# Expert lists written to DRAM by indirect DMAs in place of one-hots and their products, in a two-expert-per-token kernel on Trainium2

## The reference

```
x = x + layernorm(attention(layernorm(x)))
xf = layernorm(x)                         # 4096 x 256
shared = (silu(xf @ sg.T) * (xf @ su.T)) @ sd.T
probs = softmax(xf @ gate_w.T)            # 8 experts
topw, topi = top_k(probs, 2); topw /= topw.sum()
routed = sum over e of  ffn_e(xf) * weight of e for the token (0 if e is not chosen)
x = x + layernorm(shared + routed)        # hidden size of each expert 704
```

## Time and profile before

| | |
|---|---|
| median of 3 runs | 873.82 us (873.72 to 875.32) |
| profiled execution | 874.38 us, of which the span of instructions 872.6 us |
| PE / DVE / ACT / POOL busy | 785.9 / 586.8 / 486.2 / 290.8 us |
| mean granted TensorE clock | 0.978 |
| batches 1 to 6 | about 42.9 us each |
| last batch, from 332.10 to 364.70 | 32.6 us |
| TAIL to the first routed tile | 364.70 to 420.10 us |
| 39 routed tiles and the end | 420.1 to 872.6 us |

### The profile page before, as it was taken

One profiled execution on the slowest core, in us unless ns is written; L12 is line 12 of the kernel. 1 busy time (PEld: TensorE's weight loads), 2 busy tenths in 40 slices (PEclk: granted clock), 3 DMA queues, 4 the chain that ended last, 5 costly groups with the idle time before them and its releaser, 6 DMA issues.

```text
span 872.6 us, 21123 instructions
## 1 busy us (share of the span) xinstructions
PE 785.9 (90%) x6605; PEld 634.1 (73%) x6606; DVE 586.8 (67%) x1585; ACT 486.2 (56%) x1062; POOL 290.8 (33%) x316
## 2 busy tenths in 40 slices
PE   2689999999999998666799999999999999999991
PEld 1346677777777766554588888888888888888880
DVE  7368797979797977898577644455555555555552
ACT  1255757574848486632266655565656565656562
POOL 3010000000010100034255555555555555555542
PEclk9989999999999999999899999999999999999995
DMA  4105262636363634330334454646464646464633
GB/s 187 48 25 188 74 205 75 199 84 195 74 200 91 183 85 140 100 82 19 80 57 68 74 98 76 123 75 146 73 145 73 145 73 145 73 143 74 145 42 94
DMA packets 115747, 93.25 MB, mean 107 GB/s; under 512 B 76816, under 2 KB 107280, under 8 KB 114512
## 3 DMA queue, kind: packets, MB, share of 16 engines
q1 hardware_dynamic: 100704, 71.60, 28.3%
q0 software_dynamic: 14976, 20.78, 16.0%
HBM read 48.70 MB, written 27.39 MB: 87 GB/s over the span
## 4 chain that ended last, share of the span: by engine, by line
PE 72%; DVE 17%; ACT 5%; issue 3%; DMA 2%; POOL 1%; ACTq 0%; SPq 0%; DVEq 0%; POOLq 0%
PE ps L910 40%; PE ps L925 18%; PE ps L981 5%; PE ps L1016 3%; DVE wgu L1270 3%; PE ps L975 2%; DVE hf L1210 2%; ACT wgu L772 2%; DVE wdn L1270 1%; PE ps L986 1%; DVE hT L1220 1%; DVE st L1382 1%; DVE wdn L1515 1%; PE ps L1020 1%; ACT silu L724 1%
## 5 line engine op out<-in xcount | busy, mean ns | idle before, releaser
L910 PE MATMUL ps<-xhl,wgu 128*128 128x256 f16 x3102 | 384.9, 274 | 12.7 <-DMA xhl<-attw 6.7
L910 PEld LDWEIGHTS ps<-xhl,wgu 128*128 (+1 forms) x3102 | 302.7, 98 | 54.5 <-issue 8.6
L1210 DVE SCALAR_TENSOR_TENSOR hf<-ps,sc,silu 128x256 f32<-128x256 f32 x330 | 159.6, 484 | 194.5 <-ACT silu L724 165.3
L925 PE MATMUL ps<-wdn,hT 128*128 (+1 forms) x1870 | 254.9, 273 | 13.6 <-DVE hT L1220 11.2
L724 ACT ACTIVATE silu<-ps,sc 128x256 f32<-128x256 f32 x275 | 130.0, 473 | 233.4 <-PE ps L910 233.2
L925 PEld LDWEIGHTS ps<-wdn,hT 128*128 128x128 f16 x1870 | 179.8, 98 | 40.6 <-DVE hT L1220 13.4
L673 POOL DMA_INDIRECT acc_d<-ysb,gst x78 | 128.9, 1652 | 44.5 <-POOL gst L669 30.9
L606 POOL TENSOR_TENSOR rstd<-ve,mhalf 128x4 f32<-128x4 f32 (+1 forms) x32 | 30.6, 959 | 315.5 <-DVE ve L1195 293.1
L738 ACT CAST hT<-hf 128x256 f16<-128x256 f32 x275 | 109.4, 398 | 14.4 <-DVE hf L1210 11.8
L1220 DVE TENSOR_TENSOR hT<-hf,hT 128x256 f16<-128x256 f32 x275 | 114.7, 417 | 1.7
L662 POOL DMA_INDIRECT attw<-xn_d,gst x78 | 80.5, 1032 | 44.4 <-POOL gst L658 32.6
(11 more groups left out here) (241 smaller groups left out, 753.2 us busy)
## 6 DMA issues: line engine op xcount, KB each, us to landing
wgu<-in_gu SPq DMA_DIRECT2D x8, 1408.0 KB, 6.1
att<-in_x SPq DMA_DIRECT2D x16, 512.0 KB, 5.4
wdn<-in_dn SPq DMA_DIRECT2D x8, 768.0 KB, 8.5
x_d<-att SPq DMA_DIRECT2D x8, 512.0 KB, 2.9
xn_d<-wgu SPq DMA_DIRECT2D x8, 512.0 KB, 3.4
acc_d<-ysb SPq DMA_DIRECT2D x16, 256.0 KB, 2.3
att<-x_d SPq DMA_DIRECT2D x8, 512.0 KB, 4.7
att<-acc_d SPq DMA_DIRECT2D x7, 512.0 KB
```

The costliest lines, as they stand in the source:

```text
L910: ins = te.matmul(o, slot_gu(slot, hw, k, j), x(hx, k), start=(n == 0), stop=(n == len(TERMS) - 1))
L925: ins = te.matmul(y_bank(u, tt), h(hh), slot_dn(slot, c, hw), start=(c == 0 and n == 0 and tt == 0), stop=(c == FC - 1 and n == 1 and tt = ...
L1210: v.scalar_tensor_tensor(out=hf[lo:P, c % 2 * TW:(c % 2 + 1) * TW], in0=up, scalar=scale_of(slot, 1, lo, P), in1=silu[lo:P, c % 2 * TW:(c ...
```

## The change

Token numbers are written to lists in DRAM. `list_d` has for each expert a list with room for all 4096 tokens, and blocks of padding behind. At the start it is filled with numbers of padding rows (4 DMAs from SP), and `xn2_d` gets 256 padding rows.

- Routing goes in three parts (PART): token tiles 0 to 15 in batch 4, 16 to 27 at the beginning of batch 7, 28 to 31 in TAIL. `ranks` on PE gives a token's rank among its expert's tokens: one fp32 product with `upper`, one with `ones` for each earlier batch's counts and one for each tile of the part but the last (1 + 0 + 15, 1 + 4 + 11 and 1 + 7 + 3 products). `route_places` on DVE adds the list's start and takes each choice's place.
- `put_on_lists` on POOL: for each of the 32 token tiles two indirect DMAs that write 128 token numbers of 4 bytes (64 in all). They stand in batches 5 and 6, in batch 7 and in TAIL.
- The first tile of each expert has fixed places in its list: SP reads these eight tiles' numbers with two DMAs when all 64 writes have landed. The numbers of the 31 later tiles are gathered by POOL, four indirect DMAs behind each scatter of tiles 2 to 9 (three behind the last of them).
- The order of the tiles is worked out on DVE during routed tiles 0 to 2 (`ordering`). `idx` serves gather and scatter.
- One-hots, inversion, `route_slots` to `route_indices` are gone. START, ORDER, LAST_ORDER and TAIL are written anew; the steps of the batches stay the same apart from the new ones.

The core of the diff:

```diff
+LAST_ORDER = [("ctx",), ("route_probs", 1), ("G", 0), ("G", 1), ("route_top1", 1), ("G", 2), ("H", 0), ("route_top2", 1), ("route_ranks", 1),
+         ("ctx_out",), ("G", 3), ("route_places", 1), ("H", 1), ("list", 1, 16), ("H", 2), ("D", 0), ("list", 1, 17), ("H", 3), ("H", 4),
+         ("list", 1, 18), ("G", 4), ("D", 1), ("channel_stats",), ("group_mean",), ("G", 5), ("list", 1, 19), ("group_var",), ("H", 5),
+         ("ctx_norm",), ("list", 1, 20), ("H", 6), ("D", 2), ("list", 1, 21), ("list", 1, 22), ("G", 6), ("H", 7), ("H", 8), ("G", 7),
...
-PROGRAM += [(b, step) for b in range(1, B - 1) for step in ORDER if b < NPRE or not step[0].startswith("prep")]
+PROGRAM += [(b, step) for b in range(1, B - 1) for step in ORDER
+            if (b < NPRE or not step[0].startswith("prep")) and (b == PART_IN or not step[0].startswith("route"))
+            and (step[0] != "list" or b == PART_IN + 1 + step[2] // (2 * NT))]
...
+            sp.wait_ge(fill_made, 1)
+            blocks = list_d.rearrange("(n c) o -> n (c o)", c=TW)
+            sp.dma_start(blocks[0:P, :], fill[:, 0:TW]).then_inc(list_filled, 16)
+            sp.dma_start(blocks[P:EMPTY + NTILE, :], fill[0:EMPTY + NTILE - P, 0:TW]).then_inc(list_filled, 16)
+            for t in range(TT):
+                sp.dma_start(xn2_d[TOK + t * P:TOK + (t + 1) * P, :], fill.bitcast(F32)).then_inc(list_filled, 16)
...
+                store_weights(n)
+
+
+            first_tiles = list_d[0:E * TOK, :].rearrange("(e n p h) o -> p e n (h o)", e=E, p=P, h=TT)[:, :, 0, :]
+            idx3 = idx[:, 0:E * TT].rearrange("p (i h) -> p i h", h=TT)
+            sp.wait_ge(listed, 16 * 2 * NTB)
+            sp.dma_start(idx3[:, 0:2, :], first_tiles[:, 0:2, :]).then_inc(idx_first, 16)
+            sp.dma_start(idx3[:, 2:E, :], first_tiles[:, 2:E, :]).then_inc(idx_rest, 16)
...
+            def put_on_lists(n, j):
+
+                pool.wait_ge(places_made, n + 1)
+                if j == 0:
+                    pool.wait_ge(list_filled, 4 * 16)
+                passed(pool)
+                for m in range(2):
+                    at = m * NTB + j
+                    g.indirect_dma_start(list_d, bass.IndirectOffsetOnAxis(ap=posi[:, at:at + 1], axis=0), tok_i[:, j:j + 1], None).then_inc(listed, 16)
 
...
+            def idx_of(i):
+
+                g.indirect_dma_start(idx[:, i * TT:(i + 1) * TT], None, list_d.rearrange("(n h) o -> n (h o)", h=TT),
+                                     bass.IndirectOffsetOnAxis(ap=table[:, i - E:i - E + 1], axis=0)).then_inc(idx_late, 16)
+
             for i in range(E + GROUP):
+                if i + 3 >= E:
+                    pool.wait_ge(idx_late, 16 * (i + 4 - E))
                 gather_x(i + 3, (i + 1) % 2, False)
                 scatter(i)
+                if i == 2:
+                    pool.wait_ge(table_made, 1)
+                    passed(pool)
+                for n in range(E + 4 * (i - 2), min(E + 4 * (i - 1), NTILE)):
+                    if i >= 2:
+                        idx_of(n)
+            pool.wait_ge(idx_late, 16 * (NTILE - E))
             with pool.Fori(0, B - 2) as b:
                 for j in range(GROUP):
...
+            def ranks(n):
+
+                a, b = PART[n]
+                pe.wait_ge(m_made, n + 1)
+                m = part_arrays(n)[4].rearrange("p (t e) -> p t e", e=E)
+                at = max_ps[:, 2 * P:2 * P + (b - a) * E].rearrange("p (t e) -> p t e", e=E)
+                te.matmul(at, upper[:, :], m, start=True, stop=False)
+                for c in range(a // NT):
+                    te.matmul(at, ones[:, :], picks[:, c * E:(c + 1) * E].rearrange("p (o e) -> p o e", o=1).to_broadcast([P, b - a, E]), start=False, stop=False)
+                for j in range(b - a - 1):
+                    ins = te.matmul(at[:, j + 1:, :], ones[:, :], m[:, j:j + 1, :].to_broadcast([P, b - a - 1 - j, E]), start=False, stop=(j == b - a - 2))
+                ins.then_inc(ranked, 1)
...
+                if kind == "route_places":
+                    a, b = PART[n]
+                    dve.wait_ge(ranked, n + 1)
+                    rl(v.tensor_tensor(te8(xx), max_ps[:, 2 * P:2 * P + count * E].rearrange("p (t e) -> p t e", e=E),
+                                       list_start.rearrange("p (o e) -> p o e", o=1).to_broadcast([P, count, E]), ALU.add))
+                    for m, oh in enumerate((o1, o2)):
+                        rl(v.tensor_tensor(cc, oh, xx, ALU.mult))
+                        rl(v.tensor_reduce(posf[:, m * NTB + a:m * NTB + b], te8(cc), AX.X, ALU.add))
+                    v.tensor_copy(posi.rearrange("p (m j) -> p m j", m=2)[:, :, a:b], posf.rearrange("p (m j) -> p m j", m=2)[:, :, a:b]).then_inc(places_made, 1)
```

More of the change, by code:

```diff
@@ L629, in _ @@
                     root(LN2, b, NT)
+                if step[0] == "list":
+                    put_on_lists(step[1], step[2])
             for step in TAIL:
-                if step[0] == "one_hots":
-                    pool.wait_ge(remainders_made, 1)
-                    if step[1] == 0:
-                        pool.wait_ge(prep_lo, NPRE * NG)
-                        x1_ready(pool, B - 1)
-                    wait(pool, onehot_used, step[1] - OHR + 1)
-                    for h in range(OHB - POOL_H, OHB):
-                        j = OHB * step[1] + h
-                        for m in range(2):
-                            n = m * NTB + j
-                            ins = g.tensor_scalar(oh_lo[step[1] % OHR][:, m, h, :], iota16[:, :], lof[:, n:n + 1], tokf[:, j:j + 1], ALU.is_equal, ALU.mult)
-                        ins.then_inc(onehot_lo_made, 1)
-            pool.wait_ge(idx_made, 2)
+                if step[0] == "list":
+                    put_on_lists(step[1], step[2])
+            pool.wait_ge(idx_first, 16)
             pool.wait_ge(xn2_stored, B * 16)
-            pool.wait_ge(comb_stored, 16)
+            pool.wait_ge(comb_stored, 3 * 16)
             def gather_x(i, r, first):
@@ L957, in _ @@
                     ffn_step(kind, step[1], 2 * b - 2, b)
+                if kind == "route_ranks":
+                    ranks(step[1])
                 if kind == "ln1_stats" and b < 0:
@@ L1090, in expert_of @@
             def expert_of(i):
+                if isinstance(i, int) and i == E:
+                    pe.wait_ge(eid_made, 1)
                 return pe.value_load(eid[0:1, bass.ds(i, 1)], min_val=1, max_val=E)
@@ L1286, in by_tile @@
                 return a.rearrange("p (t o) -> p t o", o=1).to_broadcast([P, a.shape[-1], E])
-            ends, base_, start = (small[:, 128 + 8 * n:136 + 8 * n] for n in range(3))
-            one8 = small[:, 184:192]
+            list_start, base_ = small[:, 184:192], small[:, 136:144]
             def route(kind, n):
                 count = PART[n][1] - PART[n][0]
-                lg, pr, df, o1, o2, mm, cc, xx = (part_of(arr, n) for arr in (logits[:, :], r_p, r_t, r_o1, r_o2, r_m, r_c, r_x))
+                lg = part_of(logits[:, :], n)
+                pr, df, o1, o2, mm, cc, xx = part_arrays(n)
                 m1, m2, mr, ms = (part_of(small[:, NTB * m:NTB * (m + 1)], n, 1) for m in range(4))
-                w1, w2 = (part_of(wts[:, NTB * m:NTB * (m + 1)], n, 1) for m in range(2))
+                w1, w2 = m1, m2
                 rev_b = rev[:, :].rearrange("p (o e) -> p o e", o=1).to_broadcast([P, count, E])
@@ L1339, in _ @@
                 kind = step[0]
+                if kind == "H" and b == 1 and step[1] == 0:
+                    dve.wait_ge(list_filled, 4 * 16)
                 if kind in "GDH":
@@ L1482, in _ @@
                     v.tensor_scalar(picked[:, NTILE:NCOL], ident[:, 0:NTILE], order[:, 5:6], None, ALU.mult).then_inc(order_made, 1)
-                if kind == "route_table":
+                if k == 4:
                     dve.wait_ge(order_spread, 1)
-                    c3 = col16.rearrange("p (i h) -> p i h", h=TT)
-                    for h in range(TT):
-                        v.tensor_scalar(c3[:, E:, h], att_ps[2][:, E:NTILE], float(TT), float(h), ALU.mult, ALU.add)
-                        v.tensor_scalar(c3[:, 0:E, h], base_, float(TT), float(h), ALU.mult, ALU.add)
+                    v.tensor_scalar(table, att_ps[2][:, E:NTILE], float(P), row_i[:, 0:1], ALU.mult, ALU.add).then_inc(table_made, 1)
@@ L1547, in lay_out @@
             def lay_out(i, c):
+                if isinstance(i, int) and (i, c) in ORDERING:
+                    ordering(ORDERING[(i, c)])
                 kind, s, n = LATE.get((i, c), ("", 0, 0)) if isinstance(i, int) else ("", 0, 0)
```

227 lines of the change are left out of this document (99 added, 128 removed), and 14 rows, old and new, of tables (LAST_ORDER, ORDER, TAIL).

## The result

The changed kernel takes 964.69 us in the median of 4 runs, the one before 874.23: ratio 1.1029 (95% interval 1.1003 to 1.1054). It is slower, as forecast, but by 90 us where the forecast had 16; the range ended at 920.

What follows compares the result with a forecast made beforehand. Attention batches had TensorE busy 41.87 and VectorE 36.57 of 42.92 us, both near full; routed tiles filled TensorE. Terms +5 + 3 - 2 + 0 + 10 = +16 us on 874.38 gave 890, range 864 to 920.

Steps and rivals of the forecast that it cites:

- Price of a list DMA: On POOL: one indirect list DMA costs 1.33 us, the gather's 1.03 plus 0.30 between two.
- rivals at 0.9 and 1.95: POOL's time per list DMA: 0.9 us gives 866 in all (chance 0.22), 1.95 us gives 930 (chance 0.13).
- the 2.1 us for the last write to land: Behind the last logits: the last list DMA lands 2.1 us after issue, from the final scatter's 3.74 less 1.62.
- b = 4, +5: Batch 4: routing of part 0 adds 33 VectorE operations, 9.9 us; batch +5 us (3 to 8).
- b = 5 and 6, +3: Batches 5 and 6: list DMAs between POOL's roots delay them and VectorE; 2.5 + 0.5 = +3 us (0 to 23).
- the lateness of the roots (5.3 and 2.7): POOL in batches 5 and 6: list DMAs make the last root 5.3 us late in b = 5, 2.7 in b = 6.
- Last batch, +20, "POOL is from here on the chain": Batch 7: after places at 341, 24 list DMAs (31.9 us) and three roots on POOL; logits 383.0, 20 us late.
- Tail, -22: Last logits to first routed tile: 35 us against 57.15, with SP's read of the numbers done at 23.7; gains 22.
- 31 reads, +10: Routed tiles 2 to 9: late reads on POOL make tiles need 13.4 us, stopping ACT and TensorE; +10 us (0 to 30).
- Rival C: Routed stage: the late reads hide behind gathers and slower tiles 2 to 4, rest as forecast; +6, 880 us; chance 0.15.
- Rivals A and B: POOL's list DMAs: A, cheap at 0.9 us, -8, 866 (chance 0.22); B, 1.95 us, +56, 930 (chance 0.13).
- "wrong if POOL shows idle time in the last batch": Batch 7: the forecast's own test, which expected POOL busy ahead of the LN2 root, some 20 us late.

Runs made afterwards that it cites:

- the padding runs: Changed kernel with all routed tiles reading padding numbers; list writes left out (896.42 us), or sent to another array 4 (999.85), 16 (927.10) or 64 bytes apart (926.16).

## Why the prediction was wrong, point by point

- **Price of a list DMA** (1.33 us, rivals at 0.9 and 1.95): right, 1.022 and 1.000 + 0.30. The case hung on something else. Each 128 writes were *issued* in 1.3 us but served more slowly. Nothing in the trace of before shows a 4-byte write beside its neighbour, and I gave no bound to their service: the 2.1 us for the last write to land were taken from the scatter of 1 KB rows. It was 13.5, and 1.2 with the writes apart. This is the step that failed, and it failed at three places: the tail, and the stores and transposes behind the writes in b = 5, 6 and 7, which I never priced. With writes 64 bytes apart 60 of the 90 us went.
- **b = 4, +5**: right, +6.2; VectorE's busy time rose by 8.2 where I had 9.9. (It came out as 49.1 to 49.5 or as 52.4 in kernels with the same code up to there, and b = 5 and 6 as 43.3 to 43.8 or as 46.4 to 46.9; not explained.)
- **b = 5 and 6, +3**: the lateness of the roots (5.3 and 2.7) was right, 6.2 and 3.6. I charged 3 of these 8 us, the chip 7.5: that much went when the writes were moved and the third root of b = 5 came 18.8 us behind the first again. The other 30 of 37.9 are the backlog.
- **Last batch, +20, "POOL is from here on the chain"**: +41.5 measured. 21.4 are backlog. The run without writes still had 16 of the other 20, so only some 4 were GpSimd's row. The rest is the routing of part 1, which stands ahead of the channel statistics. Moving it together with 22 writes gave 11.2 back and put the GN root 5.8 us behind the logits of batch 6 again. 44.5 us are then left, 6.8 below the run without writes. I had priced those VectorE steps at 11 us and then let GpSimd's row start behind them as the only chain. That my 20 matches what is left beside the backlog is luck: the size was right for the wrong engine. The stop of ScalarE is in it too: 6.94 us "remote" at 409.29 in the changed kernel.
- **Tail, -22**: -11.1 to the first copy. With writes apart it is 24.4 us from the logits to the copy, against my 23.7 + the wait; so the steps were right and the landing wrong.
- **31 reads, +10**: 13.4 by removal on two kernels, in the range of 0 to 30, with the mechanism named. GpSimd hardly waits and a tile takes 13.3 us on average (542.95 to 635.80 for seven), where I had 13.4. TensorE is idle as I had said: between 500 and 600 us it is busy for 91.63, and for 100.00 in the earlier trace rows. Rival C falls.

```profile
583.29 1.87 POOL L718 DMA_INDIRECT acc_d<-ysb,gst  x1 [1.62 <-issue]
585.47 1.62 POOL L718 DMA_INDIRECT acc_d<-ysb,gst  x1 [0.30 <-issue]
587.39 1.02 POOL L735 DMA_INDIRECT idx<-list_d,tokf  x1 [0.30 <-issue]
...
591.24 0.94 POOL L735 DMA_INDIRECT idx<-list_d,tokf  x1 [0.30 <-issue]
...
596.40 1.62 POOL L718 DMA_INDIRECT acc_d<-ysb,gst  x1 [0.81 <-POOL gst L714]
```

  From scatter to scatter 13.1 us here, with four reads between; in the earlier trace rows a tile takes 10.9 and has 2.86 of idle time.
- **Rivals A and B** both priced issue on GpSimd, so all my cases stood on one side of the cause; a rival on service was missing. The Trainium skill, "DMA: Bandwidth & Descriptors", section "Specifications", has transfers under 512 B done as read-modify-write, which could have suggested one. It doesn't name the distance between neighbours, which decided here.
- **Its own sign of error**, "wrong if POOL shows idle time in the last batch", was met: GpSimd busy for 25.98 of 76.26 us.

## What to carry to other kernels

Price a new DMA twice, its issue and its service, and where no row shows its kind (4-byte rows, neighbours in memory, many in a row), keep a rival in which everything else on the DMA queues waits behind it. Where many partitions write small neighbouring elements in one indirect DMA, permute the destination so that neighbours lie apart. 64 bytes did it here, with five more short operations on VectorE that gave back 60 us, and in the padding runs 16 bytes did as well. Put such DMAs where the issuing engine has idle time, behind the last root and ahead of the next: that was worth 7.5 us. A row of twenty in one place came with a stop of ScalarE in five kernels and with none in two, so look for it in the profile of each.
